# A graph kernel's gathered edge rows: one 32-bit product by a weighted one-hot in place of a high part and a low part

## What is computed

```python
agg = segment_sum(x[src], edge_type * n + dst, num_segments=N_REL * n)
mean = agg.reshape(N_REL, n, -1) / jnp.maximum(cnt, 1.0).reshape(N_REL, n, 1)
h1 = jnp.einsum('rni,rio->no', mean, W_rel) + x @ W_root + b_rgcn
```

## Time and profile before

| | us |
|---|---|
| median of 3 runs | 4028.89 |
| lowest and highest | 4000.62, 4031.58 |
| span of the profiled execution | 3914.8 |

### The profile page before, as it was taken

One profiled execution on the slowest core, in us unless ns is written; L12 is line 12 of the kernel. 1 busy time (PEld: TensorE's weight loads), 2 busy tenths in 40 slices (PEclk: granted clock), 3 DMA queues, 4 the chain that ended last, 5 costly groups with the idle time before them and its releaser, 6 DMA issues.

```text
span 3914.8 us, 67824 instructions
## 1 busy us (share of the span) xinstructions
PE 3517.8 (90%) x19011; PEld 2232.3 (57%) x19011; DVE 2100.5 (54%) x4163; ACT 1514.6 (39%) x2563; POOL 1651.4 (42%) x2058
## 2 busy tenths in 40 slices
PE   6877777785899999999999999999999998778888
PEld 4333336784656666666666666666666665444545
DVE  7999998776552122122122455444444533776764
ACT  2765553553412222222222344444444432444440
POOL 0766661000004554454430444444444412787771
PEclk9999997797999999999999999999999998888889
DMA  2000000001124333333333555555555544555541
GB/s 81 1 1 0 0 0 10 1 1 36 57 70 137 101 107 110 102 111 106 102 113 103 158 160 159 158 160 163 165 165 167 165 121 140 150 145 144 146 119 55
DMA packets 224477, 390.34 MB, mean 100 GB/s; under 512 B 38885, under 2 KB 179172, under 8 KB 224398
## 3 DMA queue, kind: packets, MB, share of 16 engines
q1 hardware_dynamic: 164942, 246.72, 18.6%
q0 software_dynamic: 57600, 141.81, 13.6%
q10 hardware_dynamic: 1856, 0.79, 0.1%
HBM read 250.79 MB, written 138.41 MB: 99 GB/s over the span
## 4 chain that ended last, share of the span: by engine, by line
PE 68%; DVE 14%; issue 7%; DMA 4%; POOL 3%; ACT 2%; DVEq 1%; SPq 0%; POOLq 0%; ACTq 0%
PE bank L1578 17%; PE bank L1579 17%; PE bank L1580 17%; PE bank L1462 3%; POOL arena L584 3%; DMA arena<-y_half,idx_now 3%; DVE arena L1023 3%; DVE arena L1016 2%; PE bank L1569 2%; PE bank L1635 2%; PE bank L1570 2%; PE bank L1553 2%; DVE arena L1059 2%; PE bank L1354 1%; DVE arena L1084 1%
## 5 line engine op out<-in xcount | busy, mean ns | idle before, releaser
L1578 PE MATMUL bank<-arena 128*128 128x384 f16 (+1 forms) x4200 | 1380.3, 329 | 1.1 <-ACT arena L834 1.0
L1579 PE MATMUL bank<-arena 128*128 128x384 f16 (+1 forms) x4200 | 1377.9, 328 | 0.0
L1580 PE MATMUL bank<-arena 128*128 128x384 f16 (+1 forms) x4200 | 1377.0, 328 | 0.0
L834 ACT ACTIVATE arena<-bank,winv 128x384 f32<-128x384 f32 (+1 forms) x680 | 390.4, 579 | 1287.5 <-PE bank L1580 1269.2
L584 POOL DMA_INDIRECT arena<-y_half,idx_now x720 | 771.3, 1071 | 210.6 <-issue 149.4
L1578 PEld LDWEIGHTS bank<-arena 128*128 128x128 f16 (+2 forms) x4200 | 424.9, 101 | 279.9 <-issue 26.3
L1580 PEld LDWEIGHTS bank<-arena 128*128 128x128 f16 (+2 forms) x4200 | 424.4, 101 | 265.3 <-issue 7.3
L1579 PEld LDWEIGHTS bank<-arena 128*128 128x128 f16 (+2 forms) x4200 | 425.1, 101 | 257.7 <-issue 5.8
L824 ACT ACTIVATE agg_hi<-arena,typ_s 128x384 fp32r<-128x384 f32 x720 | 414.7, 610 | 386.1 <-DMA arena<-y_half,idx_now 302.5
L1229 DVE SCALAR_TENSOR_TENSOR agg_lo<-arena,typ_s,agg_hi 128x384 fp32r<-128x384 f32 x720 | 443.6, 616 | 176.9 <-ACT agg_hi L824 171.2
L554 POOL PARTITION_ALL_REDUCE wgm<-wabs x70 | 25.4, 364 | 984.0 <-DVE wabs L1148 981.1
(11 more groups left out here) (215 smaller groups left out, 4015.9 us busy)
## 6 DMA issues: line engine op xcount, KB each, us to landing
y_half<-arena SPq DMA_DIRECT2D x612, 192.0 KB
arena<-in_L_gnn_W_rel_dram SPq DMA_DIRECT2D x68, 1152.0 KB, 7.5
arena<-y_half,idx_now POOLq DMA_INDIRECT x720, 3.5
y_half<-arena SPq DMA_DIRECT2D x68, 147.0 KB
w_now<-rel_inv_dram,idx_now POOLq DMA_INDIRECT x360, 2.7
arena<-in_x_dram SPq DMA_DIRECT2D x10, 384.0 KB, 3.4
arena<-in_L_gnn_b_rgcn_dram SPq DMA_DIRECT2D x10, 384.0 KB, 9.7
x_dram<-arena SPq DMA_DIRECT2D x9, 384.0 KB, 2.5
```

The costliest lines, as they stand in the source:

```text
L834: nc.scalar.activation(to, bank[n % RB][0:r, 0:CH], ACT.Copy, scale=winv[0:r, c:c + 1]).then_inc(r_copied, 1)
L1578: nc.tensor.matmul(acc, xh, w_hi[c][:, k, :], start=(k == 0), stop=False)
L1579: nc.tensor.matmul(acc, xh, w_lo[c][:, k, :], start=False, stop=False)
L1580: ins = nc.tensor.matmul(acc, xl, w_hi[c][:, k, :], start=False, stop=(k == KT - 1))
```

## The change

`agg_hi` and `agg_lo` are gone. The weight moves into the one-hot: DVE compares and multiplies in the same instruction and writes 32-bit floats, into eight slots instead of four. PE multiplies this one-hot by the gathered rows where they lie, as one product of 32-bit floats for each tile instead of two of the fp32r type. `edge_high` goes from ACT's program. The gather into a slot, and the copy of indices, wait for `e_sum` (PE has done the unit two back) where they waited for `e_lo` and `e_hi`; PE waits for the landing itself and for the one-hot (`e_oh`).

```diff
-        agg_oh = sb("agg_oh", [P, UT, P], F32R)
-        agg_hi = sb("agg_hi", [P, UT, CH], F32R)
-        agg_lo = sb("agg_lo", [P, UT, CH], F32R)
+        agg_oh = sb("agg_oh", [P, 2 * UT, P], F32)
...
                     if t == UT - 1:
-                        pool.wait_ge(e_hi, V * UT + UT)
+                        pool.wait_ge(e_sum, V * UT + UT)
                         next_rows(q, i, m, c + 1)
-                    pool.wait_ge(e_lo, V * UT + t + 1)
+                    pool.wait_ge(e_sum, V * UT + t + 1)
...
-            def edge_high(q, i, m, c):
-
-                V, place, uses = unit(q, i, m, c)
-                for t in range(UT):
-                    act.wait_ge(g_loaded[place * UT + t], (uses + 1) * 16)
-                    act.wait_ge(e_sum, V * UT + t + 1)
-                    nc.scalar.activation(agg_hi[:, t, :], graw[place * UT + t], ACT.Copy,
-                                         scale=w_s[:, bass.ds((i * m + c) * UT + t, 1)]).then_inc(e_hi, 1)
...
-            def edge_low(q, i, m, c):
+            def edge_rows(q, i, m, c):
...
                     dve.wait_ge(e_sum, V * UT + t + 1)
-                    nc.vector.tensor_scalar(agg_oh[:, t, :], iota[:, 0:P], dst_s[:, at], None, ALU.is_equal)
-                    dve.wait_ge(e_hi, V * UT + (t + 1 + 2 * UT))
-                    nc.vector.scalar_tensor_tensor(agg_lo[:, t, :], graw[place * UT + t], w_s[:, at],
-                                                   agg_hi[:, t, :].bitcast(F32), ALU.mult, ALU.subtract).then_inc(e_lo, 1)
+                    nc.vector.tensor_scalar(agg_oh[:, place * UT + t, :], iota[:, 0:P], dst_s[:, at], w_s[:, at],
+                                            ALU.is_equal, ALU.mult).then_inc(e_oh, 1)
...
             def edge_add(q, i, m, c, roots=0):
...
-                dve.wait_ge(e_sum, V * UT + 2 * UT)
+                dve.wait_ge(e_sum, V * UT + 3 * UT)
...
             def edge_sum(q, i, m, c):
-                V, place, _ = unit(q, i, m, c)
+                V, place, uses = unit(q, i, m, c)
...
                 for t in range(UT):
-                    pe.wait_ge(e_lo, V * UT + (t + 1 + 2 * UT))
-                    nc.tensor.matmul(acc, agg_oh[:, t, :], agg_hi[:, t, :], start=(t == 0), stop=False)
-                    nc.tensor.matmul(acc, agg_oh[:, t, :], agg_lo[:, t, :], start=False, stop=(t == UT - 1))\
-                        .then_inc(e_sum, 1)
+                    s = place * UT + t
+                    pe.wait_ge(e_oh, V * UT + t + 1)
+                    pe.wait_ge(g_loaded[s], (uses + 1) * 16)
+                    nc.tensor.matmul(acc, agg_oh[:, s, :], graw[s], start=(t == 0), stop=(t == UT - 1)).then_inc(e_sum, 1)
...
             nc.tensor.matmul(bank[7][:, 0:2], zeros[:, :], iota[:, 0:2], start=True, stop=True)\
-                .then_inc(e_sum, UT)
+                .then_inc(e_sum, 2 * UT)
```

More of the change, by code:

```diff
@@ L300, in program @@
         g_loaded = [sem(f"g_loaded{i}") for i in range(2 * UT)]
-        e_hi, e_lo, e_sum, e_added = sem("e_hi"), sem("e_lo"), sem("e_sum"), sem("e_added")
+        e_oh, e_sum, e_added = sem("e_oh"), sem("e_sum"), sem("e_added")
         wg_loaded, scaled, uT_psum, uT_ready, share_psum, share_ready = (sem(n) for n in (
@@ L339, in program @@
         AGG_PAIRS = UNITS // (2 * PER)
-        SPLIT_AT = [1, 4, 7][:PER]
         UNIT_AT = [4, 7, 10][:PER]
@@ L834, in copy_out @@
                 nc.scalar.activation(to, bank[n % RB][0:r, 0:CH], ACT.Copy, scale=winv[0:r, c:c + 1]).then_inc(r_copied, 1)
[L836 to L842, removed]
             nc.scalar.copy(credit[:, 3:4], ones[:, 0:1]).then_inc(r_copied, RB)
@@ L845, in _ @@
             for q in range(HALVES):
[L846 to L852, removed]
+                with act.Fori(0, PAIRS - 1) as i:
                     for j in range(2):
-                        one_step(q, i, j, False)
+                        for n in range(NT):
+                            copy_out(q, i, j, n)
                         high(q, i + 1, j)
                 for j in range(2):
-                    one_step(q, PAIRS - 1, j, False)
+                    for n in range(NT):
+                        copy_out(q, PAIRS - 1, j, n)
                     high(q + 1, 0, j)
@@ L882, in piece_out @@
                     sums_out(0, j)
-            with act.Fori(0, PARTS * ROOTS) as i:
-                edge_high(HALVES - 1, i, 2, 0)
-                edge_high(HALVES - 1, i, 2, 1)
             for m in range(len(PIECES)):
[L888 to L892, removed]
+                piece_out(m)
             for kind, j in FINAL:
@@ L1240, in edge_add @@
                 nc.vector.tensor_tensor(hs_flat[:, o], hs_flat[:, o], bank[SUMS + place][:, 0:CH], ALU.add).then_inc(e_added, 1)
-            nc.vector.memset(credit[:, 4:5], 0.0).then_inc(e_lo, 2 * UT)
             nc.vector.memset(credit[:, 5:6], 0.0).then_inc(e_added, 2)
@@ L1249, in _ @@
                     dve.wait_ge(hs_set, 16 * NT)
+                    dve.wait_ge(edge_w, UNITS)
                     with dve.Fori(0, AGG_PAIRS) as i:
@@ L1252, in _ @@
                             for k in range(PER):
-                                edge_low(q - 1, i, 2 * PER, j * PER + k)
+                                edge_rows(q - 1, i, 2 * PER, j * PER + k)
                                 if k == PER - 1:
@@ L1287, in last_part @@
                 for c in range(PART):
-                    edge_low(q, i, PART, c + 1)
+                    edge_rows(q, i, PART, c + 1)
                     edge_add(q, i, PART, c, i * ROOTS + sum(at <= c for at in ROOT_AT))
@@ L1291, in last_part @@
                         root_add(i, ROOT_AT.index(c + 1))
-            edge_low(HALVES - 1, 0, PART, 0)
+            edge_rows(HALVES - 1, 0, PART, 0)
             dve.wait_ge(deg_sqrt, 1)
@@ L1300, in _ @@
             with dve.Fori(0, REST // 2 - 1) as i:
-                edge_low(last, i, 2, first + 1)
+                edge_rows(last, i, 2, first + 1)
                 edge_add(last, i, 2, first, 2 * NT)
-                edge_low(last, i, 2, first + 2)
+                edge_rows(last, i, 2, first + 2)
                 edge_add(last, i, 2, first + 1, 2 * NT)
-            edge_low(last, 0, 2, UNITS - 1)
+            edge_rows(last, 0, 2, UNITS - 1)
             edge_add(last, 0, 2, UNITS - 2, 2 * NT)
```

## The result

The changed kernel takes 4095.09 us, the median of four runs (4069.24 to 4097.11), where the kernel before took 4028.63 in four runs beside it (4000.62 to 4031.58). The ratio is 1.0154, with an interval of 1.0121 to 1.0187: slower by 1.5%, 66 us.

What follows compares the result with a forecast made beforehand. It took PE to bound the fused steps and POOL's issuing of gathers the tail; 103 - 24 - 1 = +78 us, added to the median before, gave 4107 us, 2% slower, range 4070 to 4165.

Steps and rivals of the forecast that it cites:

- Fused steps, +103: Fused steps: a unit's products cost full PE 2.57 us, 1.14 more than now, +103 us for 90 units.
- the 35 and 38 that were named as signs of being wrong: Fused steps: under 35 us a step means a cheaper product; over 38, a late gather or costly type changes.
- What was costed at nothing: Fused steps: ACT's and DVE's savings, the one-hot's second scalar and POOL's new wait were taken as worth nothing.
- the rival with the late gather: Fused steps: slots come free only behind PE, so gathers are late; 2 us in 30 steps, 4167 us; chance 0.05.
- the one with the half-price product: Fused steps: the 32-bit product costs half, a unit 1.30 us; 3986 to 3992 us in all; chance 0.03.
- Tail, -24: Tail: POOL's gathers speed up once line 1229 goes; -24 us taken, between 0 and -31.
- the rival by which the tail gives nothing back: Tail: something other than line 1229 lengthens gathers, or units pay for type changes; 4131 to 4160 us; chance 0.10.
- The tail gets longer with gathers that wait for PE: Tail: named as a sign that the prediction is wrong; 460 to 466 us was expected from first to last gather.
- PE's clock in the tail: Tail: with PE busy 403 of about 465 us, the granted clock was expected above 0.93, from 0.84.
- PE as the prompt tail's bound: Tail: rival that PE becomes the bound through its clock; 4125 us at 0.84, 4170 at 0.75; chance 0.20.
- The end, -1: Very end: the chain from the last landing loses ACT's 0.61 and DVE's 0.62, PE's 0.36 becomes 0.64; -1 us.
- The median before lies 114 us over the span, which covers what lies around it: Whole kernel: the sum from the profiled span, 3914.8 us, was added to the median as it stood.

Runs made afterwards that it cites:

- e11_after: The changed kernel without an edit, on the fifth chip, against the kernel before: 3986.22 us, ratio 1.0192.
- e4_hybrid_dve: Kernel before with only the tail changed to the one 32-bit product, DVE waiting for the landing: 3970.85 us, 0.9943 of before.
- e5_hybrid_pe: Kernel before with only the tail changed to the one 32-bit product, PE waiting for the landing: 3963.96 us, 0.9925 of before.
- e6_contention: e5_hybrid_pe plus, behind each tail one-hot, a DVE instruction of the removed kind that nobody waits for: 3933.45 us, 1.0024 of before.
- e2_after: The changed kernel without an edit, on the third chip, against the kernel before: 3999.61 us, ratio 1.0163.
- e8_before: The kernel before without an edit, on the fourth chip: 3990.75 us.
- e9_hybrid_pe: The kernel of e5_hybrid_pe without a further edit, on the fourth chip: 3966.7 us, 0.9941 of before.
- e12_light_tail: The changed kernel with most of PE's root products and pieces left out of the tail, edge sums whole: 3979.66 us, 1.0175 of before.
- e0_before: The kernel before without an edit, traced again on the second chip: 3995.96 us.
- e1_dve_waits: The changed kernel with DVE, not PE, waiting for a landing, ahead of the one-hot: 4070.6 us, 1.0201 of before.
- e10_slots: e9_hybrid_pe with sixteen places for gathered rows in the tail instead of eight, on the fourth chip: 3969.47 us, 0.9939 of before.

## Why the prediction was right, and where it was wrong

**The sign and the time.** 4107 was forecast for a measured 4095.09, 12 us off, and +78 for a measured +66. The span of the prediction was 3993 against the page's 3914.8; the execution that can be laid beside that page is e11_after (prompt, and like it in the first layer), 3987.0. By stages it is +0.4 up to the fused steps, +99.5 in them, -24.1 in the tail, -3.6 behind it: +72 for the forecast +78.

**Fused steps, +103: right, the mechanism and the size.** A step is 36.99 us where 36.9 to 37.1 stood, and 30 x (36.99 - 33.55) = 103.2. Records are 0.322 us apart, so a unit pays nothing for changing types. In e4_hybrid_dve and e5_hybrid_pe the cost went with the new product. The stage grew by 99.5 and not 103 because the step that a count of equal steps leaves out differs: the first fused step of before took 38.47 us, of e11_after 36.72. All 2.7 us of PE's wait for `agg_lo` in the earlier trace rows lie in it, at a granted clock of 0.91 for the 38 us around it. The prediction took the growth of one later step thirty times, and so missed what was special in the first.

On the changed kernel's own page, a late execution, two lines 777 are 34.61 to 39.37 us apart, outside the 35 and 38 that were named as signs of being wrong. Their mean over 29 steps is 36.91 and PE was busy for 1105 of 1109 us of the stage, so the cost is the same: it is ACT's place in the step that moves there, and the signs were drawn for prompt signals.

**What was costed at nothing: right.** The new one-hot costs DVE 0.283 us against 0.300, inside its bounds and hidden. No gather is late (PE waited 1.9 us). So the rival with the late gather is out, as is the one with the half-price product: 0.322 us is a record, and there are two.

**Tail, -24: right where signals are prompt,** -23.6 and -24.1 (465.1 and 464.6 against 488.7, with 460 to 466 forecast); e6_contention shows the mechanism by itself. But the size is in part luck. The terms were -25 for the gathers, -4 for the copies, -3 for waits and +4 for the one-hot's hold, which is -28; the -24 that was taken has 4 us more off, which no row prices. Measured on e2_after, the gathers gave 22.3, the copies 3.5, and the idle time grew by 2.3: the 3 us of waits didn't come back. The one-hot's own hold of the gathers was put at 4 us: a mean of 0.963 us against 0.955 for (3 x 0.95 + 0.97) / 4 leaves 3.

By the Trainium skill (GPSIMD Engine Reference, section Key points) GpSimd contends with vector instructions that have two SBUF inputs or run in a two-port mode. The instruction of e6_contention is of the first kind, and the trace agrees; of the second these 3 us are all that could be.

In late executions the gathers give back as much (24.0 us between e8_before and e9_hybrid_pe) but the tail 17 to 23: 561.2 to 544.1, 561.2 to 538.3, 558.0 to 536.4. So the rival by which the tail gives nothing back is out in either kind. "The tail gets longer with gathers that wait for PE" was named as a sign of being wrong, and the two pages show just that, 488.7 and 543.3. But one is prompt and the other late; like with like the tail is shorter each time.

**PE's clock in the tail: right where signals are prompt.** 0.98 where over 0.93 was forecast. In late executions it is 0.90 to 0.94, from 0.80 before, and 0.92 on the changed kernel's own page. PE as the prompt tail's bound was not seen: e12_light_tail takes a fifth of its work away for 3 us. The 403 us for PE's work there has the three pieces of 226 columns (12 us) twice; 391 is right, and nothing hung on it.

**The end, -1: mis-sized.** It is -3.6. The chain got shorter by one more thing, the clock: the last twelve records between the edge products and the long products of line 1635 went from 6.38 us to 4.03, the granted clock over them from 0.63 to 1.00. PE on the page's execution of before, then in e11_after (line 1613 was 1645):

```profile
3795.24 6.38 PE L1645 MATMUL bank<-arena 128*98 128x384 f32 x12
```

```profile
3869.80 4.03 PE L1613 MATMUL bank<-arena 128*98 128x384 f32 x12
```

**The step that failed: "The median before lies 114 us over the span, which covers what lies around it".** Only 1.7 us lie around the span (4092.4 and 4094.12). So the page of before shows a shorter kind of execution than the three timed runs were. The other 112 us must lie in the stages; where, no trace of those three runs shows, but e0_before, with 79 us more than the page, has 72 of them in the tail and 8 behind it. The tail had been priced from the page. It came out near the time since the change costs nearly the same in each kind, and that is luck: from e0_before to e1_dve_waits the tail gives back 17.1 us and what follows 11.7, from the page to e11_after 24.1 and 3.6. Two differences make the kinds, and both come with the old fused steps and with the new (e10_slots, whose fused steps are the old ones, has the long first layer too). One is the late signals: with them the tail of before is 558 to 561 us for 489, and what follows 132 to 135 for 128. The other is in the first layer. Line 957 in the first 1140 us of e11_after, then of e2_after:

```profile
L957 DVE TENSOR_SCALAR arena<-iota,arena 125x128 f16<-125x128 f16 x330 | 102.4, 310 | 8.0 <-PE bank L1339 8.0
```

```profile
L957 DVE TENSOR_SCALAR arena<-iota,arena 125x128 f16<-125x128 f16 x330 | 151.2, 458 | 8.0 <-PE bank L1339 8.0
```

The same 330 instructions took 49 us more, while line 959 beside them took 20 less (125.4 and 105.6); the fused steps begin at 2173.4 in the one and 2198.1 in the other. The runs fall into four groups by this:

| | before | changed | difference |
|---|---|---|---|
| prompt, short first layer | 3908 to 3916 | 3984 to 3989 | about +75 |
| prompt, long first layer | 3936 to 3945 | 4013 to 4014 | about +72 |
| late, short first layer (first chip) | 4000.6 | 4069.2 | +69 |
| late, long first layer (first chip) | 4028.4 to 4031.6 | 4094.1 to 4097.1 | +66 |

The grouping of runs without a profile goes by their time alone; it is argued, not shown. The 66 us of the result and the 86 of the third chip (3999.61 - 3913.24) are medians over such groups, and the second mixes two of them.

## What to carry to other kernels

- Where an engine is full, price a replacement by the time between starts of that very shape elsewhere in the trace, and count the records for one instruction; the busy engines beside it don't matter. Here twelve instructions of ACT and twelve of DVE in a step were bought off with 3.4 us of PE, the one engine that had none to spare, and the same edit pays where PE has slack: apply it stage by stage (0.9925 to 0.9943, and 0.9881 with sixteen slots on a chip with prompt signals).
- Before pricing from one profiled execution, compare its span with the median of the runs: a gap of 3% is not an overhead around it but a sign that it shows another kind of execution than those timed.

## What the runs showed of the hardware that I had not expected

- **PE's signals can arrive late.** In every profile from the second and the fourth chip and on the changed kernel's page, in both kernels, semaphore events of PE's products came late, in the place shown 4.7 us behind the product's end, several at once, 0.04 us apart. On the third and fifth chip no event was over 0.02 us late. In e0_before it is so in the fused steps too, where nobody needs them soon. Where an engine waits for each, as in this tail, it costs about 70 us of 560. It isn't PE's own wait for a landing (e1_dve_waits), and sixteen slots don't help; in e10_slots the one-hots stand behind a late signal in DVE's program. What causes it, and whether PE's root work has part in it, stays open.
- **PE's granted clock in the tail rose, and neither PE's busy share nor DVE's load tells why.** It went from 0.84 to 0.98, as PE's busy share went from 0.78 to 0.89 (e2_after). In e12_light_tail PE's share was 0.73, less than before, and the clock still 0.98. In e6_contention DVE was as busy as before, and the clock 0.97. ACT was idle in all three; whether that has part in it isn't tested.
- **A DVE instruction that POOL doesn't wait for costs POOL time:** 0.099 us on each gather and 0.112 on each copy (e6_contention).
- **The same 330 DVE instructions take 0.310 or 0.458 us** from one execution to the next, worth some 25 us of span, for no reason that these profiles show.
